# Half rows for two quantised weights, and a new list of steps for each engine, in a language-model tower on one core

## What is computed

```
h = w0[ids] @ w1, masked and scaled                                   # 4096 x 256
x = layernorm(h)
k, v, r = token-shift mixes of layernorm(x) times wk, wv, sigmoid(wr)
wkv = recurrence over the 256 tokens of a sequence (k, v, decay)
x = x + (r * wkv) @ wo
x = x + sigmoid(xr @ cwr) * (relu(xk @ cwk)**2 @ cwv)                 # 1024 wide
h = h + x
gate, y = q(n) @ q(w_gate).T, q(n) @ q(w_up).T      # n = layernorm(h), weights 704 x 256
h = h + q(silu(gate) * y) @ q(w_down).T             # w_down is 256 x 704
q(t): per block of 16 along the last axis, scale = max|t| / 6; t / scale to the nearest of
      0, 0.5, 1, 1.5, 2, 3, 4, 6 with its sign; times scale
```

## Time and profile before

| | us |
|---|---|
| median of 3 runs (785.11 to 786.60) | 785.88 |
| the profiled execution | 786.62 |
| its span, first to last instruction | 784.8 |
| PE busy in the span | 698.4 |
| DVE busy | 600.1 |
| ACT busy | 512.1 |

### The profile page before, as it was taken

One profiled execution on the slowest core, in us unless ns is written; L12 is line 12 of the kernel. 1 busy time (PEld: TensorE's weight loads), 2 busy tenths in 40 slices (PEclk: granted clock), 3 DMA queues, 4 the chain that ended last, 5 costly groups with the idle time before them and its releaser, 6 DMA issues.

```text
span 784.8 us, 9883 instructions
## 1 busy us (share of the span) xinstructions
PE 698.4 (89%) x3311; PEld 565.1 (72%) x3311; DVE 600.1 (76%) x1023; ACT 512.1 (65%) x889; POOL 146.7 (19%) x220
## 2 busy tenths in 40 slices
PE   4262799699999999999999999999999999699866
PEld 3231676589688977888688958897788768688664
DVE  0798745987798888788788778888878788863764
ACT  2448488578874888389757886588848974662221
POOL 2302230433023300421022302330141002200000
PEclk9676799899999999999999999999999999999999
DMA  3900000000010000100000001000010000000000
GB/s 122 255 16 27 1 28 1 28 1 28 1 41 14 27 1 14 41 1 27 14 30 13 28 14 28 15 28 0 25 30 1 1 14 15 1 0 14 14 1 28
DMA packets 11956, 19.34 MB, mean 25 GB/s; under 512 B 972, under 2 KB 9346, under 8 KB 11906
## 3 DMA queue, kind: packets, MB, share of 16 engines
q1 hardware_dynamic: 9302, 10.31, 4.4%
q0 software_dynamic: 2560, 8.39, 3.5%
q10 hardware_dynamic: 44, 0.01, 0.0%
HBM read 14.51 MB, written 4.19 MB: 24 GB/s over the span
## 4 chain that ended last, share of the span: by engine, by line
PE 69%; DVE 16%; ACT 6%; issue 6%; DMA 2%; POOL 0%; DVEq 0%; ACTq 0%; POOLq 0%; SPq 0%
PE psB L548 18%; PE psB L575 11%; PE psC L617 11%; PE psC L644 11%; PE psA L539 9%; PE psA L511 3%; PE psC L631 2%; ACT mix L798 2%; DVE top L352 1%; DVE mix L1084 1%; DMA rows<-L_tok_w,ids_now 1%; PE psB L521 1%; DMA kkT<-L_ffn_w_gate 1%; ACT take L792 1%; PE psA L499 1%
## 5 line engine op out<-in xcount | busy, mean ns | idle before, releaser
L548 PE MATMUL psB<-cwv_s,kkT 128*128 128x256 f32 x512 | 113.2, 379 | 0.0
L548 PEld LDWEIGHTS psB<-cwv_s,kkT 128*128 128x128 f32 x512 | 96.6, 190 | 16.1 <-issue 3.7
L431 POOL DMA_INDIRECT rows<-L_tok_w,ids_now x32 | 46.2, 1443 | 278.6 <-PE psA L499 266.9
L617 PE MATMUL psC<-up_hi,xq_hi 128*128 128x352 f32 x256 | 88.5, 346 | 9.0 <-DVE xq_lo L1196 8.0
L539 PE MATMUL psA<-mix,kvr_s 128*128 128x512 f32 x192 | 89.3, 611 | 6.4 <-ACT kT L768 6.4
L644 PE MATMUL psC<-downT,hqT 128*128 128x256 f32 (+1 forms) x384 | 95.0, 392 | 0.0
L644 PEld LDWEIGHTS psC<-downT,hqT 128*128 128x128 f32 (+1 forms) x384 | 68.7, 189 | 26.0 <-issue 18.8
L617 PE MATMUL psC<-up_hi,xq_lo 128*128 128x352 f32 x256 | 84.1, 329 | 0.0
L617 PE MATMUL psC<-up_lo,xq_hi 128*128 128x352 f32 x256 | 83.7, 327 | 0.0
L539 PEld LDWEIGHTS psA<-mix,kvr_s 128*128 128x128 f32 x192 | 36.9, 196 | 47.4 <-issue 46.2
L965 DVE SCALAR_TENSOR_TENSOR mix<-hT,rest,mix 128x512 f32<-128x512 f32 x80 | 54.3, 746 | 10.3 <-ACT mix L746 10.3
(11 more groups left out here) (163 smaller groups left out, 1431.1 us busy)
## 6 DMA issues: line engine op xcount, KB each, us to landing
out<-h SPq DMA_DIRECT2D x16, 256.0 KB, 2.1
mix<-L_attn_cwk SPq DMA_DIRECT2D x1, 1024.0 KB, 13.8
cwv_s<-L_attn_cwv SPq DMA_DIRECT2D x1, 1024.0 KB, 15.8
kkT<-L_ffn_w_gate SPq DMA_DIRECT2D x1, 704.0 KB
kkT<-L_ffn_w_up SPq DMA_DIRECT2D x1, 704.0 KB
hqT<-L_ffn_w_down SPq DMA_DIRECT2D x1, 704.0 KB, 13.4
w_s<-L_tok_w SPq DMA_DIRECT2D x1, 512.0 KB, 4.0
rows<-L_tok_w,ids_now POOLq DMA_INDIRECT x32, 4.3
```

The lines of the kernel that those rows point to most:

```text
L431: pool.indirect_dma_start(rows[:, q, :], None, tok_w0, bass.IndirectOffsetOnAxis(ap=ids_now[:, s, t:t + 1], axis=0)).then_inc(rows_in[q], 16)
L548: mm = nc.tensor.matmul(psB[:, B.slot(name), q * D:(q + 1) * D], lhsT[:, k, (2 * j + q) * P:(2 * j + q + 1) * P], weight[:, k, :], start=( ...
L617: mm = nc.tensor.matmul(psC[:, C.slot(name), f, 0:INTER // 2], a[:, k, t * P:(t + 1) * P], b[:, w, k, f * (INTER // 2):(f + 1) * (INTER // ...
```

## The change

Two things are changed.

The layout: gate's and up's weights are seen as half rows of 128 numbers, 1408 of them, in 128 partitions of 11. A partition holds 11 x 128 = 1408 numbers, which are two halves of 704. Each load now moves 1408 runs of 128 numbers (512 bytes) where it moved 704 runs of 256 (1024 bytes). `w_quant0` and `w_quant1` work on 128x704 where they worked on 88x1024. The PE turns 11 blocks of 128x128 where it turned 16 of 88x88. ACT's copies and DVE's splits take the turned half rows apart again (`turned_part`): one of 1024 and one of 384 columns, read with a step of two, where there were two of 704.

The lists: all but SP's come to another sequence.

```diff
-GP = 88
-GJ = INTER // GP
+GJ = INTER * H // P
...
-    "dve": [("c_up1", 2), ("b_low", 1), ("c_quant1", 2), ("c_up2", 2), ("w_split1", 1), ("c_quant2", 2),
...
+    "dve": [("c_split1", 4), ("b_mix", 3), ("a_stat", 2), ("c_up1", 4), ("w_par", -3), ("b_low", 3), ("w_quant2", 3),
...
-        raw_up = kkT[0:GP].rearrange("p k c -> p (k c)").rearrange("p (j d) -> p j d", d=D)
+        raw_up = kkT[:].rearrange("p k c -> p (k c)")[:, 0:2 * GJ * P].rearrange("p (j d) -> p j d", d=P)
+
+        def halves(k, n):
+
+            return kkT[:].rearrange("p k c -> p (k c)")[:, (2 * k + n) * INTER:(2 * k + n + 1) * INTER]
+
+        def turned_part(d):
+
+            first, last = 8 * d * P // H, min(8 * d + 8, GJ) * P // H
+            return slice(first, last), psC[:, d].rearrange("p b n -> p (b n)")[:, 0:(last - first) * H].rearrange("p (n h) -> p h n", h=H)
...
-                sp.dma_start(raw_up[:, k * GJ:(k + 1) * GJ, :], w.rearrange("(j p) d -> p j d", p=GP)).then_inc(s_raw[k], 16)
+                sp.dma_start(raw_up[:, k * GJ:(k + 1) * GJ, :], w.rearrange("n (h d) -> (n h) d", h=H).rearrange("(j p) d -> p j d", p=P)).then_inc(s_raw[k], 16)
...
-                            for j in range(GJ):
-                                mm = nc.tensor.transpose(psC[:, d, j // 4, (j % 4) * GP:(j % 4 + 1) * GP],
-                                                         raw_up[:, m * GJ + j, d * P:(d + 1) * P], ident[0:GP, 0:GP])
+                            for j in range(8 * d, min(8 * d + 8, GJ)):
+                                mm = nc.tensor.transpose(psC[:, d, j % 8 // 4, (j % 4) * P:(j % 4 + 1) * P],
+                                                         raw_up[:, m * GJ + j, :], ident[:])
...
-                            nc.scalar.copy(up_hi[:, m, d, :].rearrange("p (f n) -> p f n", f=2),
-                                           psC[:, d, :, 0:INTER // 2]).then_inc(s_ws, 1)
+                            there, here = turned_part(d)
+                            nc.scalar.copy(up_hi[:, m, :, there], here).then_inc(s_ws, 1)
...
-                        parts = [part(n, raw_up[:, 8 * k + 4 * n:8 * k + 4 * n + 4, :].rearrange("p j d -> p (j d)"),
-                                      square_w[n][0:GP], GP, NBW, scales_w) for n in range(2)]
+                        parts = [part(n, halves(k, n), square_w[n][:, 0:INTER], P, NB, scales_w) for n in range(2)]
```

More of the change, by code:

```diff
@@ L67 @@
 ORDER = {
[19 rows of a table removed]
-    "pool": [("gather1", 1), ("c_coef0", 3), ("c_coef1", 3), ("b_sum", 2), ("b_coef", 2), ("a_coef", 1),
-        ("gather0", 0)],
-    "sp": [("c_down1", 3), ("c_down0", 2)],
[5 rows of a table added]
+    "act": [("c_cols1", 1), ("w_par", -3), ("b_cols", 0), ("b_part", 0), ("c_up1", 1), ("a_emb1", -1),
[7 rows of a table added]
+    "dve": [("c_split1", 4), ("b_mix", 3), ("a_stat", 2), ("c_up1", 4), ("w_par", -3), ("b_low", 3), ("w_quant2", 3),
[5 rows of a table added]
+        ("b_coef", -2)],
+    "sp": [("c_down1", 2), ("c_down0", 1)],
 }
@@ L882, in step @@
                         if k < 2:
-                            src = raw_up[:, 8 * k + 4 * n:8 * k + 4 * n + 4, :].rearrange("p j d -> p (j d)")
-                            dst = square_w[n][0:GP]
+                            src, dst = halves(k, n), square_w[n][:, 0:INTER]
                         else:
@@ L1184, in step @@
                         dve.wait_ge(s_ws, 2 * m + d + 1)
-                        nc.vector.tensor_tensor(up_lo[:, m, d, :].rearrange("p (f n) -> p f n", f=2), psC[:, d, :, 0:INTER // 2],
-                                                up_hi[:, m, d, :].bitcast(F32).rearrange("p (f n) -> p f n", f=2), ALU.subtract
+                        there, here = turned_part(d)
+                        nc.vector.tensor_tensor(up_lo[:, m, :, there], here, up_hi[:, m, :, there].bitcast(F32), ALU.subtract
                                                 ).then_inc(s_wc, 1)
```

## The result

The changed kernel takes 774.88 us (median of 4 runs, 773.80 to 775.75); the kernel before took 786.24 beside it. The ratio is 0.9855, 95% interval 0.9834 to 0.9875: 11.4 us less. The forecast was 770.4, range 765.5 to 777.

What follows compares the result with a forecast made beforehand. It took the kernel as a start in which data reach PE late, then nearly unbroken PE work from the first c_cols0. Terms -15.2 + 1.7 - 2.0 = -15.5 from 786.6, less 0.7, gave 770.4 us, range 765.5 to 777.

Steps and rivals of the forecast that it cites:

- case A: Whole kernel: the forecast itself comes true, 767 to 773.5 us; chance 0.55.
- Up behind the first recurrence: Start, chunk 0: up's quantisation leaves DVE's path; step behind the scans -13.5 us, b_out0 -12.2, r costing nothing.
- gate first: Start, ACT: chunk 0's norm no longer queued behind the squares of `w_sq0`, so it begins 1.9 us earlier.
- Gate's load: Start: half rows double the packets of gate's load, so gate arrives later, +1.7 us, between -0.8 and +4.2.
- Rival B: Start: gate comes as early as DVE can use it, -18.0 in sum, 767.9 us; chance 0.18.
- The b_ stage: Chunk 0 behind the first recurrence: b_gate runs 87.7 to 91.3, key products from 107.46 to 92.0, -15.4 us.
- rival C: Start: PE's low clock or ACT's longer queue gives back some 5 us, 775.4 us; chance 0.20.
- First c_cols0: End of the start: c_cols0@0, held by ACT's copies of `w_turn2`, moves from 156.17 to 141.0, -15.2 us before the load term.
- Full periods: About six periods: `a_turn1` and `a_emb1` fill PE's waits ahead of c_cols1 and b_cols; -2 us, ends 0 and -4.
- Drain: End of the kernel: no PE work is moved; up to +0.5 us for c_sq1 behind c_up2.
- D: Full periods: r late on ACT stalls PE's a_turn0 in each of six periods, slower, 788.4 us; chance 0.04.
- E: Start: first c_cols0 hangs on w_down or ACT's copies, not the recurrence, so nothing moves, 785.9 us; chance 0.03.

Runs made afterwards that it cites:

- half_88_40: The changed kernel with its gate and up loads each cut at partition 88 (88 and 40 partitions), same bytes and packets; ran once, 774.01 us.
- fill: The changed kernel with 20 identity transposes added in two PE pauses, 6 ahead of `w_turn1` and 14 ahead of b_gate@0; 771.6 us, ratio 0.9820.
- steady: The kernel before, with PE, ACT and POOL going over to the new sequences around the first c_cols0; 787.62 us, ratio 0.9993.

## Why the prediction held, and where it did not

The range and the sign held; the median is 4.5 us above the forecast and outside the 767 to 773.5 that case A, the forecast itself, was given. The total fell into the range in part by luck, as two errors in the start cancel. By its own steps:

**Up behind the first recurrence, and gate first: right.** With gate's arrival (-1.15) taken off what was measured, since the prediction has it as a term of its own, the step behind the scans moved by -13.3 (forecast -13.5), `takev` by -12.3 (-12.4) and b_out0@0 by -11.9 (-12.2). r as a new guest cost what was said: PE's rows of chunk 1 waited for it (12.47 us at 65.12) and b_out0@0 stands behind them, 0.5 us after DVE was done.

**Gate's load: wrong, by 2.9 us.** The step was "larger packets moved faster, so packets count": the two rates also differed in the partitions, and with the same packets a cut at partition 88 halves the rate (`half_88_40`). The term is -1.15 instead of +1.7, bounded by the statistics that DVE has to finish first. Rival B, at a chance of 0.18, had the direction right; how much each of partitions and packets gives is not fully told.

**The b_ stage: the mechanism was forecast as rival C, and it came.** The sum took b_gate@0 at 3.6 us; it took 6.78. The argument against C, that a pause of 1.86 at 107.46 left products at full rate, did not carry over to two pauses of 1.16 and 2.20 close together. The forecast had room for them in its own numbers, from 83.4 to 87.7 with only `w_turn1` between. A row of the kernel before would have told more than the one at 107.46:

```profile
94.69 1.97 PE L521 MATMUL psB<-ident,mix 128*128 128x128 f32 x8 [2.91 <-ACT mix L798]
```

Behind this pause 8 transposes took 1.97 us, as against 1.09 at full clock, and `a_emb1` its 5.70. The term that failed is "it runs 87.7 to 91.3": +3.1, by `fill`; the first key product came 2.3 later than forecast, gate's arrival taken off. The slow b_gate@0 also made DVE's wait for the squares 5.34 instead of the "some 2.5" of the prediction. With the clock mended what lies behind is as forecast: in `fill` that wait is 2.30, and b_out0@1 at 134.12 is -16.0 without gate's arrival, forecast -15.8.

**First c_cols0: right, by two errors that cancel.** -13.5 was forecast with the load, -12.9 measured. -2.9 from the load and +3.0 from the clock (143.29 against 140.32 in `fill`) nearly cancel, which is luck. The copies of `w_turn2` cost 1.6 and not 0.7: the quantised chunk was ready at 141.7.

**Full periods: wrong.** -2 was forecast; the order itself gives nothing (`steady`), and the 0.6 that is gained between the first c_cols0 and the last comes from the first period, which was not in the sum. The step that failed is "a_turn1 and a_emb1 are moved into exactly these two waits": it asked what fills the wait, and not what the moved steps had covered where they stood. Its bound of 0 was in the range.

**Drain: +1.2 against at most +0.5,** not by c_sq1 but by the clock of the last product, which was slow in eight of the ten kernels with this pause, with either order. That the profile of before is one of the two at 5.93 is chance as far as the runs show.

**The rest.** The profiled execution was 0.4 below the median this time and 0.7 above it before (785.88, the median that the prediction used): 1.1. In sum 0.6 (c_cols0) + 1.4 (periods) + 1.2 (drain) + 1.1 = 4.3 of the 4.5.

**Rivals.** D did not come: in full periods no wait stands ahead of `a_turn0`. E is refuted by c_cols0@0 and the end moving together. B and C were each put as a whole case against A; both happened at once, and A's time plus the lost periods plus the clock of the drain lands near C's 775.4. That the time is C's number is a coincidence of its price.

## What to carry to other kernels

Where a start hangs on a load, count its partitions before its packets: here 512-byte pieces in 128 partitions arrived earlier than 1024-byte pieces in 88. When a step is moved into a wait, look at who will wait for what the step used to cover; in a loop without slack the wait only moves. And once an order is good, look at the product behind each pause of PE for its duration, not only at the pause: 20 transposes of the identity gave some 3 us here, more than any further move of a step.
